# Adding weighted expert rows in memory with an accumulating scatter, in place of a weighted sum after the expert loop

## The chip, the cores and the metric

One core of a Trainium2 chip runs the whole program. The metric is the device time of one execution in microseconds; the kernel before takes 620.18 us (median of 3 runs, 618.78 to 622.79).

## The reference

x has shape (8, 512, 256): 8 sequences of 512 tokens with 256 channels, float32. There are two blocks, each a residual around a normalised sublayer:

```python
x = x + LN(S4D(LN(x)))          # convolution along the sequence, done through a transform, + its own LN
x = x + LN(MoE(LN(x)))          # what this case is about
# MoE(z0):
z = LN(z0) * ln_g + ln_b
probs = softmax(z @ rW + rb)                 # 8 experts, the two best are kept
w = top2(probs) / sum(top2(probs))
hid = gelu(z @ W1[e] + b1[e])                # 256 -> 512
out_e = hid @ W2[e] + b2[e]                  # 512 -> 256
return z0 + sum over the two chosen e of w_e * out_e
```

So each of the 4096 tokens goes through two of eight experts. Before the last LN stands z0 plus two weighted expert rows, z0 being the normalised row itself.

## The kernel before, in words

**Rows and routing.** The first stage works through the 8 sequences in a pipeline (`steps`): transform, multiply, inverse transform, norms. Per sequence b it leaves `xs[b]` (x after the first block, "x1"), stored to `x1_dram` by SyncE's `store_x1`, and `zn[buf(b)]`, the normalised rows with two more columns, the token's number (column H) and its second expert (column H+1). `zn` has four buffers; ScalarE's `renormalise` writes them. VectorE's `choose` and `place` find the two experts of each token and its place in each expert's region, and GpSimd scatters `zn` into `z_rows` (L1121), 128 rows per indirect DMA. Then VectorE makes the table of 71 tiles of 128 rows (`tab`, `tab_e`), sorted by expert, each expert padded to whole tiles with rows that go to a trash area, and the softmax weights `wgt`.

**The expert loop.** `tiles(eng, part)` writes the same software pipeline for each engine: part i handles tile i+2 in its first step, i+1 in its second, i in its third and i-1 in its last. Parts -2 to 2 and the last three are written out, the others run in a hardware loop of 6 parts per turn (`UNROLL`), whose turn costs a branch and, on TensorE and VectorE, register loads of the expert's number (L295). Each engine executes its own list in order, and semaphores tie the lists together. For one part:
- TensorE: transpose the rows (L1321), first layer (L1334), transpose the hidden rows (L1343), second layer (L1353). The layers run as three products of high and low parts.
- ScalarE: `z_f`, the rows with gain and bias (L587), tile i+2; the high part of the transposed hidden rows, `h_hl` (L595), tile i; GELU (L601), tile i+1.
- VectorE: flag (L1010) and destination (L1013) of tile i+2, then the two halves of `z_hl` (L1018, L1020); `hb` = first layer + bias (L1028), tile i+1; low part of `h_hl` (L1033), tile i; index copy `dst` (L1042) and `y_sb` = second layer + bias (L1043), tile i-1.
- GpSimd: `scatter_y` writes `y_sb` by `dst` to `y_rows` (L1157), 2 x 4096 rows, first and second choice apart. Each scatter waits until the one before has landed.
- SyncE loads the next tile's rows (L383).

`gate(eng)` is an increment of a semaphore of its own that stands between a wait and the instruction after it. `do` issues an instruction and waits for its end.

**The tail.** SyncE waits for all scatters, then loads for n = 0 to 7 both choices of a sequence (`ya`, L413, 2 x 512 KB), with the 2 MB of x1 of the other four sequences in between (L411). GpSimd builds `diag`, diagonal matrices of the weights (L1171); TensorE sums the two choices with them (L1369); ScalarE has computed z0 anew from x1 into `acc` (`base`, L610); VectorE adds both (L1053), takes the statistics (L1057, L1062), ScalarE the square root (L617), VectorE scale and shift (L1067 to L1073), ScalarE normalises (L621), VectorE adds x1 (L1079), SyncE stores (L417).

## Time and profile before

| what | value |
|---|---|
| time of the profiled execution | 619.86 us |
| its span, first to last instruction | 618.0 us |
| mean granted clock of TensorE | 0.899 |
| TensorE matmuls busy | 483.4 us, 78% |
| TensorE weight loads busy | 418.9 us, 68% |
| VectorE busy | 463.6 us, 75% |
| ScalarE busy | 347.2 us, 56% |
| GpSimd busy | 223.7 us, 36% |
| moved by DMA | 69.57 MB |

The 1.9 us between span and time lie around the instructions. By the slices of the page, the first stage reaches to about 250 us, the end of routing to 290, the expert loop to 548, the tail from there to 618. Register, branch and semaphore instructions are not counted as busy. The ends of matmuls are modelled, so TensorE's starts are a better measure than its ends. A wait called "issue" is one for which the profile shows no cause.

### The profile page before, as it was taken

Reading aid. Unit: us, or ns where it says so; the run is one execution under the profiler, and the core shown is the slowest. Engines: PE = TensorE matmul, PEld = TensorE weight load, DVE = VectorE, ACT = ScalarE, POOL = GpSimd, SP = SyncE. Lnnn points to the kernel's source line nnn. Section 1 sums busy time; section 2 is a strip of 40 time slices with the busy share of each in tenths; the row PEclk is TensorE's granted clock in tenths of the full one; section 3 lists DMA queues with packets and bytes.
Section 4 is the critical chain, followed back from the end, with each engine's and each line's share of the span. In section 5 each row is a group of like instructions: output and inputs, shape, how many; then the busy total and the mean of one; then the engine's idle time right before and its main releaser. Section 6 shows DMA issues by size and latency. Waiting matters only on the chain. (4 is left out here: it accounts for less than half of the span.)

```text
span 618.0 us, 12460 instructions
## 1 busy us (share of the span) xinstructions
PE 483.4 (78%) x2841; PEld 418.9 (68%) x2842; DVE 463.6 (75%) x1412; ACT 347.2 (56%) x751; POOL 223.7 (36%) x195
## 2 busy tenths in 40 slices
PE   0379899869979774131999999999999999947860
PEld 0129888759868673130798898888888988946740
DVE  6998787997886963864677777777778777732885
ACT  6992755654855567431555555555555555560584
POOL 0000666337675763652032232232232322342410
PEclk9997999989989975555899999999999999987885
DMA  6206600101111788245522222222222222219833
GB/s 173 102 0 250 227 1 1 68 2 69 43 53 43 274 270 286 94 133 143 175 75 80 68 77 77 68 81 72 68 76 77 69 79 74 60 45 367 300 148 136
DMA packets 37260, 69.57 MB, mean 113 GB/s; under 512 B 7568, under 2 KB 23696, under 8 KB 36720
## 3 DMA queue, kind: packets, MB, share of 16 engines
q1 hardware_dynamic: 30752, 51.48, 25.7%
q0 software_dynamic: 6480, 17.77, 8.1%
q8 instruction: 11, 0.18, 0.1%
q14 instruction: 17, 0.14, 0.1%
HBM read 42.02 MB, written 27.21 MB: 112 GB/s over the span
## 5 line engine op out<-in xcount | busy, mean ns | idle before, releaser
L1157 POOL DMA_INDIRECT y_rows<-y_sb,dst x71 | 74.6, 1051 | 195.5 <-DVE y_sb L1043 145.2
L1334 PE MATMUL psum<-ws,z_hl 128*128 x426 | 119.7, 417 | 0.6 <-DVE z_hl L1020 0.6
L1353 PE MATMUL psum<-ws,h_hl 128*128 x852 | 116.2, 286 | 0.0
L1353 PEld LDWEIGHTS psum<-ws,h_hl 128*128 128x128 f32 x852 | 103.8, 189 | 0.2 <-issue 0.2
L1121 POOL DMA_INDIRECT z_rows<-zn,pos x64 | 73.4, 1147 | 41.5 <-DVE pos L881 25.0
L1334 PEld LDWEIGHTS psum<-ws,z_hl 128*128 128x128 f32 x426 | 76.7, 192 | 15.8 <-issue 1.3
L595 ACT CAST h_hl<-psum 128x512 fp32r<-128x512 f32 x71 | 41.7, 587 | 74.0 <-PE psum L1343 73.8
L1028 DVE TENSOR_TENSOR hb<-psum,b1r 128x512 f32<-128x512 f32 x71 | 49.1, 692 | 35.9 <-issue 33.4
L587 ACT ACTIVATE z_f<-psum,gb 128x128 f32<-128x128 f32 x142 | 57.0, 451 | 15.6 <-PE psum L1321 13.6
L601 ACT ACTIVATE hg<-hb 128x512 f32<-128x512 f32 x71 | 44.9, 632 | 35.3 <-DVE hb L1028 34.6
L1224 PE MATMUL psum<-pm,ft 128*128 128x256 f32 x256 | 60.5, 396 | 0.4 <-DVE tmp L840 0.4
L1253 PE MATMUL psum<-yf,it 128*128 128x256 f32 x256 | 59.4, 387 | 0.0
L1224 PEld LDWEIGHTS psum<-pm,ft 128*128 128x128 f32 x256 | 50.4, 199 | 8.3 <-issue 1.1
L1253 PEld LDWEIGHTS psum<-yf,it 128*128 128x128 f32 x256 | 48.6, 194 | 6.5 <-POOL yf L1108 0.2
L1033 DVE TENSOR_TENSOR h_hl<-psum,h_hl 128x512 fp32r<-128x512 f32 x71 | 48.4, 681 | 0.7 <-ACT h_hl L595 0.7
L1369 PE MATMUL psum<-ya,diag 128*128 (+1 forms) x128 | 34.5, 437 | 17.8 <-DMA ya<-y_rows 11.9
L1321 PE MATMUL psum<-ident,z_in 128*128 128x128 f32 x142 | 28.5, 283 | 20.4 <-DMA z_in<-z_rows 18.6
L1369 PEld LDWEIGHTS psum<-ya,diag 128*128 128x128 f32 x128 | 28.1, 222 | 24.0 <-issue 19.2
L1343 PE MATMUL psum<-ident,hg 128*128 128x128 f32 x284 | 42.7, 273 | 0.0
L1343 PEld LDWEIGHTS psum<-ident,hg 128*128 128x128 f32 x284 | 35.5, 141 | 10.0 <-issue 0.2
L1106 POOL TENSOR_TENSOR yf<-yf,tmp 128x512 f32<-128x512 f32 x16 | 20.4, 1276 | 40.8 <-DVE rs L933 24.3
L1114 POOL TENSOR_TENSOR pm<-xn 128x512 f32<-128x512 f32 x8 | 10.3, 1287 | 67.4 <-ACT xn L444 67.4
(205 smaller groups left out, 850.2 us busy)
## 6 DMA issues: line engine op xcount, KB each, us to landing
z_in<-z_rows SPq DMA_DIRECT2D x71, 129.0 KB
w_raw<-in_dram SPq DMA_DIRECT2D x16, 512.0 KB, 5.5
ya<-y_rows SPq DMA_DIRECT2D x16, 512.0 KB, 6.1
xs<-in_dram SPq DMA_DIRECT2D x8, 512.0 KB, 5.7
x_dram<-xs SPq DMA_DIRECT2D x8, 512.0 KB
out_dram<-acc SPq DMA_DIRECT2D x8, 512.0 KB, 2.6
b1r<-in_dram SPq DMA_DIRECT2D x8, 256.0 KB
x1m<-x_dram SPq DMA_DIRECT2D x4, 512.0 KB
```

The source lines that it names most:

```text
L587: last = nc.scalar.activation(z_f[:, k], ps_z[q][:, k], ACT.Identity, bias=gb[:, 1, k:k + 1], scale=gb[:, 0, k:k + 1])
L601: nc.scalar.activation(hg[q][:, :], hb[:, :], ACT.Gelu).then_inc(sem("hg_ready"), 1)
L1028: V.tensor_tensor(hb[:, :], ps_h[q], b1r[:, bass.ds(e, 1)].rearrange("p a f -> p (a f)"), ALU.add).then_inc(sem("hb_ready"), 1)
L1033: V.tensor_tensor(h_hl[q][:, 1], ps_t[q], h_hl[q][:, 0].bitcast(F32), ALU.subtract).then_inc(sem("h_split"), 1)
L1121: pool.indirect_dma_start(z_rows, bass.IndirectOffsetOnAxis(ap=pos[row.par][:, i // 4, i % 4:i % 4 + 1], axis=0), zn[buf(row.b)][:, i % 4] ...
L1157: pool.indirect_dma_start(y_rows, bass.IndirectOffsetOnAxis(ap=dst[q][:, 0:1], axis=0), y_sb[q][:, :], None).then_inc(sem(f"y_out{q}"), 16)
L1224: last = TE.matmul(fw[u][c][:, k], ft[:, c, t, kt * P:(kt + 1) * P], pm[row.b][:, c, t], start=t == 0, stop=t == 1)
L1253: last = TE.matmul(iv[c][:, j * H:(j + 1) * H], it[:, c, k, j * P:(j + 1) * P], yf[row.par][:, c, k], start=k == 0, stop=k == KT - 1)
L1334: last = TE.matmul(ps_h[q], z_hl[q][:, a, k], w_at(e1, c, k * F, F), start=n == 0, stop=n == 5)
L1343: last = TE.transpose(ps_t[q][:, k], hg[q][:, k * P:(k + 1) * P], ident[:, :])
L1353: last = TE.matmul(ps_y[q], h_hl[q][:, a, k], w_at(e2, c, 1024 + k * H, H), start=n == 0, stop=n == 11)
L1369: last = TE.matmul(ps_mix[par][:, k * H:(k + 1) * H], diag[par][:, c, k], ya[:, bass.ds(n, 1), c, k].rearrange("p a h -> p (a h)"), start= ...
```

## The change

The sum over the two experts is made in memory. `y_rows` now has 4096 rows (and two trash blocks of 128), and SyncE stores the normalised rows z0 there in the first stage (`store_rows`). Its order changes: the stores no longer come after the last forward transform; expert 4's weights come after expert 5's. The softmax weights are stored to a small table `w_rows` (4 bytes per token and choice). In the loop, GpSimd gathers the 128 weights of tile t+4 after the scatter of tile t (`gather_w`), with the index `widx` that VectorE writes; ScalarE multiplies `y_sb` by them into `yw` (three buffers) as a fourth step for tile i-2; and GpSimd's scatter adds `yw` to the rows in memory. The two choices of a token lie in different experts, so two scatters of the same expert never meet in a row. VectorE computes for each tile (`order`) whether it may follow the scatter two back, or, at a change of expert, must wait until the one before has landed. ScalarE's first loop turn is written out (`peel`). The tail loads the finished sums once (`yr`), takes the statistics, normalises, adds x1 on GpSimd (the last half block on VectorE). The mean and variance and the shift lie in PSUM. `diag`, the mix on TensorE, `base`, and the two additions before the statistics are gone.

```diff
-TRASH = 2 * B * T
+TRASH = B * T
...
-    dest = at("dest", [P, TILES + 1], U32, c0 + 6240)
-    dst = [at(f"dst{i}", [P, 1], U32, c0 + 6528 + 32 * i) for i in range(2)]
+    dst = [at(f"dst{i}", [P, 1], U32, o0 + 71 * KB + 256 + 32 * i) for i in range(6)]
+    row_of = at("row_of", [P, TILES + 1], U32, o0 + 71 * KB + 448)
+    order = at("order", [1, TILES + 1], I32, o0 + 71 * KB + 736)
+    widx = [at(f"widx{i}", [P, 1], U32, o0 + 71 * KB + 32 * i) for i in range(2)]
+    wt = [at(f"wt{i}", [P, 1], F32, o0 + 71 * KB + 64 + 32 * i) for i in range(6)]
+    yw = [at(f"yw{i}", [P, H], F32, o0 + k * KB) for i, k in enumerate((69, 70, 49))]
...
+    mvm = [bank(i)[:, 0:8].rearrange("p (k c) -> p k c", k=4) for i in range(2)]
+    m_shift = [bank(2 + i)[:, 0:4] for i in range(2)]
...
-    y_rows = nc.dram_tensor("y_rows", [TRASH + P, H], F32, kind="Internal").ap()
+    y_rows = nc.dram_tensor("y_rows", [B * T + 2 * P, H], F32, kind="Internal").ap()
+    w_rows = nc.dram_tensor("w_rows", [2 * B * T, 1], F32, kind="Internal").ap()
...
-    def tiles(eng, part):
+    def tiles(eng, part, peel=0):
         loaded[eng.engine.name] = {}
-        for i in range(-2, 3):
+        for i in range(-2, 3 + UNROLL * peel):
             part(i, i % 2, i)
-        with eng.Fori(0, (TILES - 5) // UNROLL) as j:
+        with eng.Fori(peel, (TILES - 5) // UNROLL) as j:
...
+    def slot(t, u, ahead):
+        return (t if isinstance(t, int) else u + 3 + ahead) % UNROLL
...
+            def store_rows(lo, hi):
+                for b in range(lo, hi):
+                    sp.wait_ge(sem("x1_ready"), b + 1)
+                    sp.dma_start(x1_dram[:, b], xs[b][:, :, :]).then_inc(sem("x1_stored"), 16)
+                    sp.wait_ge(sem("zn_ready"), b + 1)
+                    sp.dma_start(y_tok[:, b], zn[buf(b)][:, :, 0:H]).then_inc(sem(f"zn_stored{buf(b)}"), 16)
+                sp.wait_ge(sem("x1_stored"), 16 * hi)
+            store_rows(0, 4)
+            load_expert(sp, 5)
+            store_rows(4, 5)
             sp.wait_ge(sem("kf_mm"), 2)
             sp.wait_ge(sem("fwd_mm"), 16)
             load_expert(sp, 4)
...
+            for q in range(2):
+                sp.dma_start(y_rows[TRASH + q * P:TRASH + q * P + P, :], zpad[:, 0:H]).then_inc(sem("trash_set"), 16)
...
+            sp.wait_ge(sem("wgt_ready"), 1)
+            sp.dma_start(w_rows.rearrange("(c p n) o -> p c (n o)", c=2, p=P),
+                         wgt[:, 0:2].rearrange("p c b k -> p c (b k)")).then_inc(sem("w_stored"), 16)
...
             for n in range(B):
-                if n >= 2:
-                    sp.wait_ge(sem(f"y0_in{n % 2}"), 16 * (n // 2))
-                    sp.wait_ge(sem(f"y1_in{n % 2}"), 16 * (n // 2))
-                if n == 3:
+                if n == 2:
+                    sp.wait_ge(sem("x1_in"), 64)
                     sp.dma_start(x1m[:, 0:4], x1_dram[:, 0:4]).then_inc(sem("x1_in"), 16)
-                for c in (1, 0):
-                    sp.dma_start(ya[:, n, c], y_tok[:, B - 1 - n, c].rearrange("p (k h) -> p k h", k=4)).then_inc(
-                        sem(f"y{c}_in{n % 2}"), 16)
+                sp.dma_start(yr[:, n], y_tok[:, B - 1 - n]).then_inc(sem(f"y_in{n}"), 16)
             for n in range(B):
                 sp.wait_ge(sem("m_out"), n + 1)
+                if n == B - 1:
+                    sp.wait_ge(sem("m_last"), 1)
...
+                    act.wait_ge(sem(f"zn_stored{row.par}"), 8 * (row.b - row.par))
...
+                t, q = i - 2, par
+                if live(t):
+                    act.wait_ge(sem("y_ready"), t + 1)
+                    gate(act)
+                    act.wait_ge(sem(f"w_in{q}"), (t - q) * 8 + 16)
+                    m = slot(t, u, -2)
+                    if not early(t, 3):
+                        act.wait_ge(sem(f"y_out{1 - q}"), (t - 2 + q) * 8)
+                    nc.scalar.activation(yw[m % 3][:, :], y_sb[q][:, :], ACT.Identity, scale=wt[m][:, 0:1]).then_inc(sem("yw_ready"), 1)
+            tiles(act, part, 1)
+            part(TILES + 1, (TILES + 1) % 2, TILES + 1)
...
+            def close(n):
+                act.wait_ge(sem("m_var"), n + 1)
+                nc.scalar.activation(rm[:, n % 2, 0, :], mvm[n % 2][:, :, 1], ACT.Sqrt, bias=eps[:, 0:1]).then_inc(sem("m_sd"), 1)
...
+                    last = nc.scalar.activation(acc[:, n, k], yr[:, n, k], ACT.Identity,
+                                                bias=rm[:, n % 2, 2, k:k + 1], scale=rm[:, n % 2, 1, k:k + 1])
+                    if n == B - 1 and k == 1:
+                        last.then_inc(sem("m_fin"), 1)
...
+            do(V.tensor_tensor(tf[0:1, 1, 1:NT], tab_e[0:1, 1:NT], tab_e[0:1, 0:NT - 1], ALU.is_equal))
+            do(V.scalar_tensor_tensor(tf[0:1, 2, 1:NT], tf[0:1, 1, 1:NT], -16.0, iot[0:1, 2, 1:NT], ALU.mult, ALU.add))
+            V.tensor_scalar(order[0:1, 1:NT], tf[0:1, 2, 1:NT], 16.0, None, ALU.max).then_inc(sem("order_ready"), 1)
...
+                    if q:
+                        V.scalar_tensor_tensor(row_of[:, bass.ds(t, 1)], z_in[q][:, H + 1:W], 0.0, z_in[q][:, H:H + 1], ALU.min, ALU.add)
+                    else:
+                        V.tensor_copy(row_of[:, bass.ds(t, 1)], z_in[q][:, H:H + 1])
                     V.tensor_scalar(flag[:, :], z_in[q][:, H + 1:W], tab_e[:, bass.ds(t, 1)], float(B * T),
                                     ALU.is_equal, ALU.mult).then_inc(sem("flag_set"), 1)
                     dve.wait_ge(sem("flag_set"), t + 1)
-                    V.tensor_tensor(dest[:, bass.ds(t, 1)], z_in[q][:, H:H + 1], flag[:, :],
+                    if not early(t, 2):
+                        dve.wait_ge(sem(f"w_in{q}"), (t - q) * 8)
+                    gate(dve)
+                    V.tensor_tensor(widx[q][:, :], z_in[q][:, H:H + 1], flag[:, :],
                                     ALU.add).then_inc(sem("dest_ready"), 1)
...
-                        dve.wait_ge(sem(f"y_out{q}"), (t - q) * 8)
+                        dve.wait_ge(sem("yw_ready"), t - 1)
                     gate(dve)
-                    V.tensor_copy(dst[q][:, :], dest[:, bass.ds(t, 1)])
+                    V.tensor_copy(dst[slot(t, u, -1)][:, :], row_of[:, bass.ds(t, 1)])
...
+            def spread_of(n):
+                dve.wait_ge(sem(f"y_in{n}"), 16)
+                if n > 1:
+                    dve.wait_ge(sem("m_sd"), n - 1)
...
+                    last = V.bn_stats(st[:, n % 4, k, :], yr[:, n, k])
+                do(last)
                 for k in range(4):
+                    last = V.bn_aggr(mvm[n % 2][:, k, :], st[:, n % 4, k, :])
                 last.then_inc(sem("m_var"), 1)
...
+            def scale(n):
+                par = n % 2
+                dve.wait_ge(sem("m_sd"), n + 1)
+                if n > 1:
+                    dve.wait_ge(sem("m_fin"), n - 1)
+                do(V.reciprocal(rm[:, par, 1, :], rm[:, par, 0, :]))
+                do(V.tensor_tensor(m_shift[par], mvm[par][:, :, 0], rm[:, par, 1, :], ALU.mult))
+                V.tensor_tensor(rm[:, par, 2, :], xb[:, B - 1 - n], m_shift[par], ALU.subtract).then_inc(sem("m_rs"), 1)
+            spread_of(0)
+            for n in range(B):
+                if n + 1 < B:
+                    spread_of(n + 1)
+                scale(n)
+            dve.wait_ge(sem("m_fin"), B + 1)
             dve.wait_ge(sem("x1_in"), 80)
-            with dve.Fori(1, B // 2 - 1) as j:
-                mix(j * 2 + 2, 0)
-                scale(j * 2 + 1, 1)
-                add(j * 2)
-                mix(j * 2 + 3, 1)
-                scale(j * 2 + 2, 0)
-                add(j * 2 + 1)
-            scale(B - 1, 1)
-            add(B - 2)
-            add(B - 1)
+            V.tensor_tensor(acc[:, B - 1, 2:4], acc[:, B - 1, 2:4], x1m[:, 0, 2:4], ALU.add).then_inc(sem("m_last"), 1)
...
+            def gather_w(t, q, m):
+                pool.wait_ge(sem("dest_ready"), t + 1)
+                gate(pool)
+                pool.indirect_dma_start(wt[m][:, 0:1], None, w_rows,
+                                        bass.IndirectOffsetOnAxis(ap=widx[q][:, 0:1], axis=0)).then_inc(sem(f"w_in{q}"), 16)
+            def scatter_y(t, q, m):
                 if not early(t):
-                    pool.wait_ge(sem(f"y_out{1 - q}"), (t + q) * 8)
+                    behind = pool.value_load(order[0:1, bass.ds(t, 1)], min_val=16, max_val=16 * TILES)
+                    pool.wait_ge(sem(f"y_out{1 - q}"), behind)
+                    gate(pool)
+                if not early(t, 2):
+                    pool.wait_ge(sem(f"y_out{q}"), (t - q) * 8)
+                    gate(pool)
+                pool.wait_ge(sem("yw_ready"), t + 1)
                 gate(pool)
-                pool.indirect_dma_start(y_rows, bass.IndirectOffsetOnAxis(ap=dst[q][:, 0:1], axis=0),
-                                        y_sb[q][:, :], None).then_inc(sem(f"y_out{q}"), 16)
-            scatter_y(0, 0)
-            with pool.Fori(0, (TILES - 1) // 2) as j:
-                scatter_y(j * 2 + 1, 1)
-                scatter_y(j * 2 + 2, 0)
-            def weights(n, par):
-                if not early(n, 2):
-                    pool.wait_ge(sem("m_sum"), n - 1)
-                w = wgt[:, 0:2, bass.ds(back(n), 1)].rearrange("p c a k -> p c (a k)")
-                G.tensor_tensor(diag[par][:, :, :, :], ident[:, :].unsqueeze(1).unsqueeze(1).to_broadcast([P, 2, 4, P]),
-                                w.unsqueeze(3).to_broadcast([P, 2, 4, P]), ALU.mult).then_inc(sem("m_diag"), 1)
-            pool.wait_ge(sem("rsm_ready"), 1)
-            pool.wait_ge(sem("hb_ready"), TILES)
-            weights(0, 0)
-            weights(1, 1)
-            with pool.Fori(1, B // 2) as j:
-                weights(j * 2, 0)
-                weights(j * 2 + 1, 1)
+                pool.indirect_dma_start(y_rows, bass.IndirectOffsetOnAxis(ap=dst[m][:, 0:1], axis=0),
+                                        yw[m % 3][:, :], None, compute_op=ALU.add).then_inc(sem(f"y_out{q}"), 16)
+            pool.wait_ge(sem("w_stored"), 16)
+            for t in range(4):
+                gather_w(t, t % 2, t % 6)
+            for b in range(B - 2):
+                pool.wait_ge(sem(f"zn_stored{b % 2}"), 16 * (b // 2 + 1))
+            for i in (2, 3):
+                pool.wait_ge(sem(f"zn_stored{i}"), 16)
+            pool.wait_ge(sem("trash_set"), 32)
+            pool.wait_ge(sem("order_ready"), 1)
+            for t in range(7):
+                scatter_y(t, t % 2, t % 6)
+                gather_w(t + 4, t % 2, (t + 4) % 6)
+            with pool.Fori(1, (TILES - 5) // UNROLL) as j:
+                for u in range(UNROLL):
+                    scatter_y(j * UNROLL + (1 + u), (1 + u) % 2, (1 + u) % 6)
+                    gather_w(j * UNROLL + (5 + u), (1 + u) % 2, (5 + u) % 6)
+            for t in range(TILES - 4, TILES):
+                scatter_y(t, t % 2, t % 6)
+            def add(n, ks):
+                pool.wait_ge(sem("m_fin"), n + 1)
+                if n % 4 == 0:
+                    pool.wait_ge(sem("x1_in"), 80 if n else 64)
+                G.tensor_tensor(acc[:, n, ks], acc[:, n, ks], x1m[:, B - 1 - n, ks], ALU.add).then_inc(sem("m_out"), 1)
+            for n in range(B):
+                add(n, slice(0, 2 if n == B - 1 else 4))
```

## Rows read from the trace of the kernel before

**Rows 1.** Busy time by stretch: busy us (instructions) per engine, granted clock, DMA share, GB/s.

```profile
450.00:500.00 50.00, 49.66 (x338) 44.19 (x337) 39.34 (x114) 27.87 (x58) 14.61 (x14) 1.00 0.24 74
...
560.00:570.00 10.00, 9.63 (x33) 8.13 (x34) 3.01 (x9) 0.02 (x1) 1.90 (x1) 0.73 1.01 376
```

**Rows 2.** ScalarE's longest wait in the loop, 330 to 530: total us, times, longest.

```profile
ACT h_hl L595 <- PE psum L1343: 60.4, 57, 1.2
```

**Rows 3.** Timeline of VectorE in the loop: start us, length us, instruction, idle before it.

```profile
430.48 0.69 DVE L1028 TENSOR_TENSOR hb<-psum,b1r 128x512 f32<-128x512 f32 x1 [0.49 <-issue]
...
439.48 0.15 DVE L1042 COPY dst<-dest 128x1 uint32 x1 [0.42 <-issue]
...
441.65 0.69 DVE L1028 TENSOR_TENSOR hb<-psum,b1r 128x512 f32<-128x512 f32 x1 [0.51 <-issue]
...
443.27 0.20 DVE L1010 TENSOR_SCALAR flag<-z_in,tab_e 128x1 f32<-128x1 f32 x1
...
443.74 0.29 DVE L1018 CAST z_hl<-z_f 128x256 fp32r<-128x256 f32 x1
...
444.99 0.69 DVE L1028 TENSOR_TENSOR hb<-psum,b1r 128x512 f32<-128x512 f32 x1 [0.50 <-issue]
...
451.79 0.69 DVE L1028 TENSOR_TENSOR hb<-psum,b1r 128x512 f32<-128x512 f32 x1 [0.51 <-issue]
```

**Rows 4.** Timeline of ScalarE in the loop.

```profile
442.38 0.63 ACT L601 ACTIVATE hg<-hb 128x512 f32<-128x512 f32 x1 [0.60 <-DVE hb L1028]
442.91 0.79 ACT L587 ACTIVATE z_f<-psum,gb 128x128 f32<-128x128 f32 x2
```

**Rows 5.** Timeline of the TensorE weight loads in the loop.

```profile
440.88 1.45 PEld L1353 LDWEIGHTS psum<-ws,h_hl 128*128 128x128 f32 x12
...
444.32 1.45 PEld L1353 LDWEIGHTS psum<-ws,h_hl 128*128 128x128 f32 x12
```

**Rows 6.** ScalarE on 128x256: four in a row; a group: busy us, mean ns.

```profile
259.21 2.08 ACT L519 ACTIVATE zn<-xs,rs 128x256 f32<-128x256 f32 x4
...
L467 ACT ACTIVATE tq<-qt,phase 128x256 f32<-128x256 f32 x16 | 6.5, 493 | 0.0
```

**Rows 7.** Timeline of GpSimd outside and in the loop, with the y_sb it waits for.

```profile
274.06 0.98 POOL L1121 DMA_INDIRECT z_rows<-zn,pos  x1 [0.30 <-issue]
...
446.37 0.42 DVE L1043 TENSOR_TENSOR y_sb<-psum,b2r 128x256 f32<-128x256 f32 x1
...
447.61 1.12 POOL L1157 DMA_INDIRECT y_rows<-y_sb,dst  x1 [2.29 <-DVE y_sb L1043]
```

**Rows 8.** DMA of L1157 from 380 to 540 us, and of L413: issue to landing.

```profile
L1157 POOL DMA_INDIRECT y_rows<-y_sb,dst x46: 958/1074/1131, 380.4 to 539.6; - x46
...
DMA to landing us min/median/max: 2.4/2.5/2.7
...
DMA to landing us min/median/max: 3.7/6.1/11.5
```

**Rows 9.** Timeline of the tail, and GpSimd on half a block (L1106).

```profile
555.21 5.83 SPq L413 DMA_DIRECT2D ya<-y_rows  x6
...
568.02 1.40 DVE L1057 BATCH_NORM_STATS2 st<-acc 128x6 f32<-128x256 f32 x4
...
569.98 0.30 ACT L617 ACTIVATE rm<-mvm,eps 128x4 f32<-128x4 f32 x1 [12.69 <-DVE mvm L1062]
...
610.62 0.28 ACT L617 ACTIVATE rm<-mvm,eps 128x4 f32<-128x4 f32 x1
...
611.45 0.16 DVE L1073 TENSOR_TENSOR rm<-rm,xb 128x4 f32<-128x4 f32 x1 [0.15 <-DVE rm L1069]
...
611.65 2.07 ACT L621 ACTIVATE acc<-acc,rm 128x256 f32<-128x256 f32 x4 [0.76 <-DVE rm L1073]
613.76 1.23 DVE L1079 TENSOR_TENSOR acc<-acc,x1m 128x1024 f32<-128x1024 f32 x1 [1.00 <-ACT acc L621]
...
L1106 POOL TENSOR_TENSOR yf<-yf,tmp x16: 1265/1277/1286, 81.5 to 215.8; 128x512 f32<-128x512 f32 x16
```

More of the change, by code:

```diff
@@ L179, in program @@
     tf = at("tf", [P, 3, TILES + 1], F32, o0 + 63 * KB)
[L180 to L182 removed]
+    iot = at("iot", [P, 3, TILES + 1], F32, o0 + 65 * KB)
+    yr = at("yr", [P, B, 4, H], F32, 0)
     acc = at("acc", [P, B, 4, H], F32, 64 * KB)
@@ L277, in back @@
         return n * -1 + (B - 1)
-    ps_mix = [bank(2 * i, 2) for i in range(2)]
+    y_tok = y_rows[0:TRASH, :].rearrange("(p b k) h -> p b k h", b=B, k=4)
     def route(b):
@@ L572, in _ @@
             act.wait_ge(sem("pad_set"), 1)
-            nc.scalar.activation(rsm[:, 0], mv1[:, :, :, 1], ACT.Sqrt, bias=eps[:, 0:1], scale=1.0 / H).then_inc(sem("rsm_sd"), 1)
             act.wait_ge(sem("wsm_sub"), 1)
@@ L601, in part @@
                     nc.scalar.activation(hg[q][:, :], hb[:, :], ACT.Gelu).then_inc(sem("hg_ready"), 1)
-            tiles(act, part)
-            def base(n):
-                b = back(n)
-                for k in range(4):
-                    last = nc.scalar.activation(acc[:, bass.ds(n, 1), k].rearrange("p a h -> p (a h)"),
-                                                x1m[:, bass.ds(b, 1), k].rearrange("p a h -> p (a h)"), ACT.Identity,
-                                                bias=rsm[:, 1, bass.ds(b, 1), k], scale=rsm[:, 0, bass.ds(b, 1), k])
-                last.then_inc(sem("m_base"), 1)
@@ L615, in close @@
-            def close(b, par):
-                act.wait_ge(sem("m_var"), b + 1)
-                nc.scalar.activation(rm[:, par, 0, :], mvm[par][:, :, 1], ACT.Sqrt, bias=eps[:, 0:1]).then_inc(sem("m_sd"), 1)
-                act.wait_ge(sem("m_rs"), b + 1)
-                for k in range(4):
-                    row = acc[:, bass.ds(b, 1), k].rearrange("p a h -> p (a h)")
-                    last = nc.scalar.activation(row, row, ACT.Identity,
-                                                bias=rm[:, par, 2, k:k + 1], scale=rm[:, par, 1, k:k + 1])
-                last.then_inc(sem("m_fin"), 1)
@@ L1182, in _ @@
+            for n in range(B):
+                add(n, slice(0, 2 if n == B - 1 else 4))
         @block.tensor
@@ L1358, in _ @@
             tiles(pe, part)
-            def mix(n, par):
-                pe.wait_ge(sem("m_diag"), n + 1)
-                pe.wait_ge(sem(f"y1_in{par}"), n * 8 + 16 - 8 * par)
-                pe.wait_ge(sem(f"y0_in{par}"), n * 8 + 16 - 8 * par)
-                if not early(n, 2):
-                    pe.wait_ge(sem("m_mixed"), n - 1)
-                for k in range(4):
-                    for c in (1, 0):
-                        last = TE.matmul(ps_mix[par][:, k * H:(k + 1) * H], diag[par][:, c, k],
-                                         ya[:, bass.ds(n, 1), c, k].rearrange("p a h -> p (a h)"),
-                                         start=c == 1, stop=c == 0)
-                last.then_inc(sem("m_sum"), 1)
-            pe.wait_ge(sem("y_ready"), TILES)
-            mix(0, 0)
-            mix(1, 1)
-            with pe.Fori(1, B // 2) as j:
-                mix(j * 2, 0)
-                mix(j * 2 + 1, 1)
 def fine(i):
```

100 lines of the change are left out of this document (16 added, 84 removed).

## Prediction

> **What bounds the kernel now.** The time busy by stretch comes first. It shows two stages that the change touches: the loop over 71 tiles, with TensorE busy all the time at full clock, and the tail, in which the DMA queues are full [rows 1]. The waits of the loop come next: ScalarE waits for TensorE, 60.4 us in 57 times [rows 2], while TensorE has no row of note. TensorE's share alone would say that nothing else matters there. The timelines say otherwise. TensorE's second layer starts every 3.44 us [rows 5]. VectorE repeats after 3.34 us where it does not stand for TensorE (its hb add starts at 441.65 and 444.99), and six tiles, one turn of the unrolled loop, take 451.79 - 430.48 = 21.31 us, or 3.55 each; that is 0.6 more than six times 3.44, spent at the turn of the loop [rows 3].
>
> The 3.34 us are a ring of two engines, read off one after the other [rows 3, 4]: hb add at 441.65, GELU at 442.38 (0.73), z_f at 442.91 (0.53), its two halves done and the cast on VectorE at 443.74 (0.83), the next hb add at 444.99 (1.25). Each waits for the one before it, by data or by its place in its engine's program. So it has 0.10 us of slack against TensorE, although ScalarE's busy share is only 56%. A new instruction between GELU and z_f goes into this ring.
>
> **The change, part by part.**
> *Weighting on ScalarE.* One 128x256 Identity with a scale per partition per tile stands at the end of ScalarE's part, after GELU and ahead of the next z_f: in the ring. Four such operations with bias and scale take 2.08 us where one takes 0.59, thus 0.50 each; sixteen with bias alone take 6.5 us, 0.41 each [rows 6]. I take 0.46. The ring becomes 3.34 + 0.46 = 3.80 us, past TensorE's 3.44.
>
> *VectorE.* Per tile one more 128x1 operation (0.20, as the flag row [rows 3]) and a wait with a gate; 0.35 together. VectorE's own way from hb to the cast takes 2.09 us, as does the way over ScalarE, which grows to 2.55, so 2.44 hides under it. Once per turn VectorE loads one register more (0.42 [rows 3]) and takes the branch: these are not hidden any more, 0.3 and 0.2. The turn is 6 x 3.80 + 0.5 = 23.3 us, 2.0 more than now.
>
> *GpSimd.* Now one indirect DMA per tile; then two, four gates and a register load. A gated scatter starts 0.82 us after its data (y_sb is done at 446.79, it starts at 447.61); two without gates follow each other with 0.30 between them [rows 7]. So a gate with its wait costs some 0.54. The queue's own work per tile is 1.07 + 0.30 + 1.07 + 0.30 = 2.7 us of issuing; the gates and the load (4 x 0.54 + 0.5) add as much again if nothing overlaps (5.4 us), nothing if all is hidden (2.7). I take 3.6, because a wait can be worked on while an indirect DMA is made, as the landing waits are now.
>
> *A second ring, through the gathered weight.* VectorE may overwrite the index of tile t only when the gather of t-2 has landed, and that gather stands behind the scatter of t-6 on the queue. Over two tiles: scatter after its weighting 0.82, gather behind it 1.3, landing 2.5 (that of the present scatter [rows 8]; a smaller transfer may need less), index and cast 0.35, then 1.25 + 0.73 + 0.53 + 0.50 to the next weighting but one. The sum is 8.0 us, 4.0 per tile, against 3.80 of the first ring. With a landing of 2.0 it is 3.74. The Trainium skill (DMA: Bandwidth & Descriptors, Anatomy of one DMA) gives a GpSimd-issued DMA some 2.0 us plus its bytes at 436 GB/s: by that 3.74 holds and the first ring decides. I go between them, 3.88 per tile, and a turn of 23.7 us: 2.4 more than now, and 2.4 x 71/6 = +28 us.
>
> *The accumulating scatter.* No row shows one. From below it lands like the plain one, 2.5 us after its start [rows 8]; from above after twice that, since each row is also read. I take 3.3. Within an expert two may be in flight, so up to 6 us would be hidden. At each of the seven changes of expert the scatter waits for the one before: 3.3, then three gates at 0.54 and 0.3 to the start, 5.2 us against 3.9, so 1.3 late, with hardly any slack in the second ring. +7 us, between 2 and 20.
>
> *GpSimd's port.* Indirect issues take 1.07 us in the loop and 0.96 to 0.98 outside it [rows 7, 8]. The Trainium skill (SBUF — State Buffer, the box on DVE blocking DMA) has a copy on VectorE lock GpSimd out of writing descriptors until it ends; the row shows 0.1 us of something like it per issue, and by the rule a second issue per tile could lose as much as the 0.29 us cast. That would only eat the slack of the queue.
>
> *Before the loop.* The normalised rows are stored once more (8 x 512 KB), two trash blocks and the weights too. The stores of x1 no longer stand behind the forward transforms. ScalarE gets four waits for them, a step or more late. All of it lies beside the rows' pipeline. The weights' store stands between the loads of the first tiles: +0.5 us.
>
> *The tail.* Now it runs from the first load of y at 555.21 to the end at 618.0, 62.8 us [rows 9]. Eight mixes on TensorE, the base on ScalarE and one addition on VectorE go; the last addition moves to GpSimd. What remains: the first 512 KB land after 3.7 us (the shortest landing [rows 8]); statistics to the square root 1.96 (568.02 to 569.98); square root to the first normalisation 1.03, less 0.11 of the 0.15 that stands ahead of L1073 behind a gate, then 2.07: the first block is normalised at 8.7. Each further block costs 2.07 + 0.92 - 0.09 of overlap = 2.9 us on ScalarE. But the 2 MB of x1 go out ahead of the third block: at 376 GB/s [rows 1] 5.6 us, so that block lands at 3.7 + 1.4 + 5.6 + 1.4 = 12.1, its statistics end at 14.0, only then is the second block scaled (VectorE's order), normalised at 16.7. Six more make 34.1. GpSimd's addition takes 2.5 us per block (1.28 for half [rows 9]), below 2.9; the last half block ends 1.2 after, and store and end take 3.0, as now from the end of the last add. Together 38.3 us, a gain of 24.5. Without the stall behind x1 it would be 29.5; with additions slowed to 3.5 us, 20. The small operands in PSUM save a gate and nothing else that a row shows.
>
> *The end of the loop.* Weighting plus a slower landing: +1.
>
> **Sum.** 619.9 of the profiled execution (0.3 below the median of 620.2): +28 +7 +0.5 +1 -24.5 = +12, **631 us**. The tail's gain is spent in the loop.
>
> **Rivals.**
> *The loop stays with TensorE's pace.* If the weighting fits into ScalarE's idle time (over 1 us before its h_hl cast, 60 us in 57 waits [rows 2]) and the gathers are early, the loop costs at most what 0.31 of extra ring costs, +10, at best nothing: 619.9 + 0 to 10 + 1.5 - 24.5 = 597 to 607 us. For it speaks the large idle time, against it that this idle time lies on the other side of z_f: it is waited out anyway after z_f has been handed over. It decides if the ring stays below 3.6.
> *GpSimd's queue becomes the pace.* If gates do not overlap with the issues (5.4 us per tile) or the accumulating scatter takes 6 us and more, a tile takes 4.5 to 5.4: (4.5 - 3.55) x 71 = +67, and +131 at the upper end: 664 to 728 us. For it: seven queue steps in place of two. Against it: 3.6 leaves 0.3. It decides from 4.0 per tile.
> *Only the first ring, no late scatters*: +24 +2 +1.5 -24.5 gives 623, within my case.
>
> **Chances.** My case, loop at 3.75 to 4.05 per tile, 0.58: its own range is 620 to 643. TensorE's pace or near it 0.22, GpSimd's 0.20. The range of 8 in 10 takes in most of both: 604 to 662. What this measurement can tell from no change is 1%, 613.9 to 626.3. Faster takes the first rival and little else, 0.23; same, the lower third of my case, 0.20; slower 0.57.
>
> **What the profile would show.** The hb adds six tiles apart stand 23 to 24.5 us apart; z_f begins later after GELU by the new ScalarE line's 0.4 to 0.5; TensorE now waits in the loop, some 0.4 us per tile, still at full clock; scatters at seven places over 5 us apart. VectorE's index operation waits for DMA. In the tail no TensorE, first store some 12 us after the first load, end 38 after it. Wrong if the turn stays at 21.3 (first rival), if GpSimd is busy or in its sequencer without a pause and the tile takes over 4.3 (second), or if the tail takes over 45: then GpSimd's additions are slower beside VectorE.

## The result

The changed kernel takes 651.9 us (median of 4 runs, 651.5 to 654.35); the kernel before 620.7 us (median of 4 runs, 618.78 to 622.79). The ratio is 1.052, with a 95% interval of 1.0485 to 1.0557: 31 us slower, where 11 were forecast (631.0 against 620.2). The time lies in the range of 604 to 662 and on the likeliest side, but above the 620 to 643 of the prediction's own case, and the slowing is nearly three times the forecast one. The profiled execution took 652.09 us, with a span of 649.9; it answers to 619.86 and 618.0 of before. The mean granted clock is 0.898 in the one and 0.899 in the other, so the clock takes no part in this comparison.

**The profile after.** First its busy time by stretch, one row from the middle of the loop and one from the tail. The columns are those of [rows 1].

```profile
450.00:500.00 50.00, 44.95 (x277) 35.99 (x277) 32.56 (x105) 25.33 (x57) 30.31 (x24) 1.00 0.37 62
620.00:630.00 10.00, 0.00 (x0) 0.00 (x0) 6.04 (x30) 5.48 (x14) 4.67 (x2) 0.50 0.99 381
```

In the loop TensorE does 277 matmuls in 50 us where it did 338 [rows 1], still at full clock. GpSimd is busy twice as long, but idle for 40%: no engine is full. In the tail TensorE has nothing to do; its clock stands at the lower level (0.50), which costs nothing there, and the DMA queues are as full as before.

The span splits at three marks: the first hb addition, the last one, and the first load of y in the tail. Times are from the trace's timelines, in us.

| stretch | before | after | difference |
|---|---|---|---|
| start to the first hb | 296.3 | 295.7 | -0.6 |
| first hb to the last (70 tiles on) | 246.8 | 300.9 | +54.1 |
| last hb to the first load of y | 12.1 | 15.1 | +3.0 |
| first load to the end | 62.8 | 38.1 | -24.7 |

The sum is +31.9, the difference of the spans. The tail gave what was forecast (-24.5). The loop cost 54 us where 28 + 7 were forecast.

**Where the loop waits.** The longest waits between 330 and 560 us, by engine, instruction and releaser: total us, times, longest.

```profile
ACT hg L613 <- DVE hb L1035: 84.2, 42, 3.3
DVE widx L1020 <- DMA wt<-w_rows,widx: 50.1, 51, 2.0
POOL y_rows L1155 <- DVE widx L1020: 40.3, 20, 2.6
```

ScalarE's wait for TensorE [rows 2] is gone from the head of the list. It now waits for VectorE's hb, and VectorE waits for a DMA, in nearly every tile: its index of tile t may be written only when the gather of t-2 has landed. GpSimd's scatter waits in turn for ScalarE's weighting and, in 20 cases by the profile, for the index. Read together these are a ring, closed over three engines and a DMA. One turn of it in the timeline, 439 to 449 us, with the instructions of the ring alone (start, length, instruction, idle before it):

```profile
439.44 0.49 ACT L622 ACTIVATE yw<-y_sb,wt 128x256 f32<-128x256 f32 x1
...
440.74 1.59 POOL L1155 DMA_INDIRECT y_rows<-yw,dst  x1 [2.14 <-ACT yw L622]
...
442.63 0.97 POOL L1141 DMA_INDIRECT wt<-w_rows,widx  x1 [0.30 <-issue]
...
445.15 0.16 DVE L1020 TENSOR_TENSOR widx<-z_in,flag 128x1 uint32<-128x1 f32 x1 [1.21 <-DMA wt<-w_rows,widx]
445.26 0.64 DVE L1025 CAST z_hl<-z_f 128x256 fp32r<-128x256 f32 x1
...
446.86 0.69 DVE L1035 TENSOR_TENSOR hb<-psum,b1r 128x512 f32<-128x512 f32 x1 [0.51 <-issue]
...
447.59 0.63 ACT L613 ACTIVATE hg<-hb 128x512 f32<-128x512 f32 x1 [2.09 <-issue]
...
448.12 0.49 ACT L622 ACTIVATE yw<-y_sb,wt 128x256 f32<-128x256 f32 x1
```

Follow it down. The weighting of one tile ends at 439.93; its scatter starts at 440.74 and holds GpSimd for 1.59 us. Only then can the gather behind it in the program be made, 442.63. It lands in time for the index at 445.15, 1.21 us after VectorE could have written it. The cast of z stands behind the index in VectorE's program and waits with it, then hb, GELU, and the next weighting but one at 448.12. That is 8.7 us from weighting to weighting, for two tiles. The two tiles of a pair are not alike: the index of one waits long for its gather (2.01, 1.76 and 1.21 us at 428.07, 436.80 and 445.15), that of the other little (0.22 and 0.64 at 431.53 and 440.68). In the timeline of VectorE just before, the hb additions stand 3.74 and 4.99 us apart.

```profile
429.44 0.69 DVE L1035 TENSOR_TENSOR hb<-psum,b1r 128x512 f32<-128x512 f32 x1 [0.51 <-issue]
...
433.18 0.69 DVE L1035 TENSOR_TENSOR hb<-psum,b1r 128x512 f32<-128x512 f32 x1 [0.50 <-issue]
...
438.17 0.69 DVE L1035 TENSOR_TENSOR hb<-psum,b1r 128x512 f32<-128x512 f32 x1 [0.51 <-issue]
```

The short one, 3.74, is the first ring with the weighting in it. The weighting's own cost is seen beside [rows 4], where z_f began 0.53 after GELU. In the timeline of ScalarE now, yw begins 0.53 after GELU and z_f another 0.40 on.

```profile
430.17 0.63 ACT L613 ACTIVATE hg<-hb 128x512 f32<-128x512 f32 x1 [3.05 <-DVE hb L1035]
...
430.70 0.49 ACT L622 ACTIVATE yw<-y_sb,wt 128x256 f32<-128x256 f32 x1
...
431.10 0.78 ACT L599 ACTIVATE z_f<-psum,gb 128x128 f32<-128x128 f32 x2
```

**The tail**, timeline rows that answer to [rows 9]:

```profile
607.89 1.55 POOL L1155 DMA_INDIRECT y_rows<-yw,dst  x1 [0.86 <-DMA y_rows<-yw,dst]
611.81 0.81 SPq L424 DMA_DIRECT2D yr<-y_rows  x2
612.67 0.42 SPq L423 DMA_DIRECT2D x1m<-x_dram  x1
613.13 3.22 SPq L424 DMA_DIRECT2D yr<-y_rows  x6
...
619.41 2.08 ACT L633 ACTIVATE acc<-yr,rm 128x256 f32<-128x256 f32 x4 [1.90 <-DVE rm L1074]
...
621.57 2.33 POOL L1181 TENSOR_TENSOR acc<-acc,x1m 128x1024 f32<-128x1024 f32 x1 [12.13 <-ACT acc L633]
623.19 1.41 DVE L1061 BATCH_NORM_STATS2 st<-yr 128x6 f32<-128x256 f32 x4 [3.81 <-DMA yr<-y_rows]
...
625.51 2.07 ACT L633 ACTIVATE acc<-yr,rm 128x256 f32<-128x256 f32 x4 [3.87 <-DVE rm L1074]
...
628.37 2.07 ACT L633 ACTIVATE acc<-yr,rm 128x256 f32<-128x256 f32 x4 [0.64 <-DVE rm L1074]
...
631.24 2.07 ACT L633 ACTIVATE acc<-yr,rm 128x256 f32<-128x256 f32 x4 [0.64 <-DVE rm L1074]
```

The third block of y comes late behind the 2 MB of x1, and VectorE stands for 3.81 us; from then on a block takes 2.87 us. The load at 611.81 stands 3.9 us behind the start of the last scatter.

### The profile page after: what moved, and what is told of

It is laid out like the page before. It is cut to its first block, busy times and chain, and to the rows that moved or that the text cites. A ratio compares the mean times of both kernels' runs of the same rounds, so it can differ in the third digit from the quotient of the medians.

```text
span 649.9 us, 12865 instructions
## 1 busy us (share of the span) xinstructions
PE 472.5 (73%) x2713; PEld 389.3 (60%) x2714; DVE 444.6 (68%) x1469; ACT 347.7 (53%) x788; POOL 335.4 (52%) x267
## 4 chain that ended last, share of the span: by engine, by line
DMA 22%; DVE 20%; issue 17%; PE 14%; ACT 13%; POOL 7%; POOLq 3%; DVEq 1%; SPq 1%; ACTq 0%
DMA y_rows<-yw,dst 11%; DMA wt<-w_rows,widx 8%; PE psum L1257 3%; POOL y_rows L1155 3%; PE psum L1228 3%; POOLq L1147 2%; ACT acc L633 2%; POOL wt L1141 2%; ACT yw L622 2%; DVE hb L1035 2%; DMA yr<-y_rows 2%; PE psum L1215 1%; ACT dump L518 1%; ACT dump L562 1%; PE psum L1204 1%
## 5 line engine op out<-in xcount | busy, mean ns | idle before, releaser
L1155 POOL DMA_INDIRECT y_rows<-yw,dst x71 | 114.1, 1607 | 106.2 <-DVE widx L1020 54.2
L1141 POOL DMA_INDIRECT wt<-w_rows,widx x71 | 70.1, 987 | 36.2 <-issue 20.9
L1020 DVE TENSOR_TENSOR widx<-z_in,flag 128x1 uint32<-128x1 f32 x71 | 11.4, 160 | 67.1 <-DMA wt<-w_rows,widx 64.3
L1257 PEld LDWEIGHTS psum<-yf,it 128*128 128x128 f32 x256 | 48.5, 194 | 6.4 <-POOL yf L1094 0.2
L1347 PE MATMUL psum<-ident,hg 128*128 128x128 f32 x284 | 44.7, 280 | 3.3 <-ACT hg L613 0.2
L1347 PEld LDWEIGHTS psum<-ident,hg 128*128 128x128 f32 x284 | 31.6, 141 | 24.1 <-ACT hg L613 20.5
```

The costliest lines, as they stand in the source:

```text
L1141: pool.indirect_dma_start(wt[m][:, 0:1], None, w_rows, bass.IndirectOffsetOnAxis(ap=widx[q][:, 0:1], axis=0)).then_inc(sem(f"w_in{q}"), 16)
L1155: pool.indirect_dma_start(y_rows, bass.IndirectOffsetOnAxis(ap=dst[m][:, 0:1], axis=0), yw[m % 3][:, :], None, compute_op=ALU.add).then_in ...
L1257: last = TE.matmul(iv[c][:, j * H:(j + 1) * H], it[:, c, k, j * P:(j + 1) * P], yf[row.par][:, c, k], start=k == 0, stop=k == KT - 1)
L1347: last = TE.transpose(ps_t[q][:, k], hg[q][:, k * P:(k + 1) * P], ident[:, :])
```

## The experiments

Three theories of the loop's 4.36 us per tile (mean distance of the hb additions from the 9th tile to the 63rd; 3.55 before). **A**: the ring weighting, scatter, gather, index, cast, hb, GELU, that is, the order of two DMAs on GpSimd's queue. **B**: the adding scatters land slowly and pace the loop themselves. **C**: GpSimd's own instructions do, its waits and gates included. Here is what the changed kernel and ten variants of it gave; "per tile" is the same mean for each. Each was timed beside the kernel before, in three groups, each on a chip of its own: e1 to e4, e5 to e8, e9 and e10. The kernel before had medians of 620.7, 620.8 and 620.8 us in them, so kernels of different groups can be set side by side. A few us of the medians are not the loop's, though: in the profiled executions the first hb addition comes between 295.7 us (after) and 301.7 (e6), though no edit changes the first stage. The granted clock is 0.97 from 100 to 200 us in before, after, e2, e3 and e7, and 0.91 to 0.93 in the others; the three latest starts (e1, e6, e10, 300.8 and later) also have only 0.95 in the first 100 us. In the loop, 300 to 540 us, it is 0.99 or 1.00 in every kernel, so the time per tile is free of it.

| kernel | edit to the changed kernel | median us (lowest to highest) | ratio to before, 95% | per tile |
|---|---|---|---|---|
| after | none | 651.9 (651.5 to 654.35) | 1.0485 to 1.0557 | 4.36 |
| e1 | six index buffers | 613.9 (612.2 to 615.9) | 0.981 to 0.994 | 3.77 |
| e2 | weighting earlier | 606.1 (605.7 to 608.0) | 0.970 to 0.983 | 3.67 |
| e3 | e1 and e2 | 604.9 (602.5 to 605.9) | 0.968 to 0.981 | 3.63 |
| e4 | scatter writes, doesn't add | 622.5 (619.6 to 625.2) | 0.9985 to 1.0056 | 3.95 |
| e5 | gather ahead of scatter | 617.4 (614.5 to 619.4) | 0.992 to 0.997 | 3.78 |
| e6 | every scatter waits for the last | 699.4 (698.1 to 701.3) | 1.121 to 1.133 | 4.90 |
| e7 | x1 behind the blocks of y | 650.5 (648.5 to 654.3) | 1.044 to 1.057 | 4.35 |
| e8 | e3 and e7 | 607.0 (605.5 to 609.9) | 0.974 to 0.985 | 3.74 |
| e9 | e3, e5 and e7 | 601.8 (594.9 to 603.8) | 0.960 to 0.975 | 3.63 |
| e10 | e3, one gate for three | 603.9 (602.9 to 606.2) | 0.970 to 0.975 | 3.65 |

**e1, six index buffers.** VectorE's write of an index waits for the gather of six tiles ago, not of two.

```
-    widx = [at(f"widx{i}", [P, 1], U32, ...) for i in range(2)]
+    widx = [at(f"widx{i}", [P, 1], U32, ...) for i in range(UNROLL)]
...
-                    if not early(t, 2):
-                        dve.wait_ge(sem(f"w_in{q}"), (t - q) * 8)
+                    m = slot(t, u, 2)
+                    if not early(t, UNROLL):
+                        dve.wait_ge(sem(f"w_in{m}"), nth(t, u, 2) * 16)
```

> Six buffers for the gather's index in place of two, each with its own semaphore; VectorE's first loop turn is written out. Theory A (the ring through the index: weighting, scatter, gather, landing, index, hb, GELU, weighting two tiles on, 8.7 us per two tiles) says that VectorE now waits for a gather three rounds back, the ring is gone and ScalarE's ring of 3.34 + 0.5 us is next: 3.85 to 3.95 us per tile, 652 - 0.45 x 70 = 620 us. Theory B (the accumulating scatters' landing paces the loop) says no change, 652. Theory C (GpSimd's own work per tile, two issues and the gates between them, paces it) says at most a few us less, 645 and over.

Measured: 613.9 us and 3.77 per tile. That is below the 3.85 to 3.95 expected, which took the weighting as 0.5 and not as 0.40. VectorE's wait for the gather is gone from the list of waits; the first ring, 3.34 + 0.40 = 3.74, is what is left. The same adding scatters and the same GpSimd instructions now run at 3.77, so neither B nor C can have set 4.36.

**e2, the weighting earlier.** ScalarE's line moves from behind GELU to behind z_f, ahead of the h_hl cast; both index buffers stay two.

```
+                t, q = i - 2, par
+                if live(t):
+                    act.wait_ge(sem("y_ready"), t + 1)
...
+                    nc.scalar.activation(yw[m % 3][:, :], y_sb[q][:, :], ACT.Identity, ...)
...
-                    nc.scalar.activation(yw[m % 3][:, :], y_sb[q][:, :], ACT.Identity, ...)
```

> Only ScalarE's weighting moves, from behind GELU to just behind z_f of the same part. Theory A: the weighting no longer stands behind hb and GELU of its part, the ring through the index now spans three tiles (about 9.5 us, 3.2 per tile) and ScalarE's own ring is back at 3.34; the loop is then paced by TensorE (3.55) or by GpSimd's shortest cycle (1.92 from scatter to gather, 1.76 from gather to scatter, 3.7 us): 608 us, between 600 and 612. Theory B: no change, 652. Theory C, if GpSimd's cycle were the pace already: 645 and over.

Measured: 606.1 us, 3.67 per tile. The edit puts the weighting behind z_f and ahead of the h_hl cast, where ScalarE stands for TensorE anyway (it still does, 26.7 us in 52 times from 330 to 560). It also starts each scatter earlier in its tile, so that the gather behind it has mostly landed when the index is due: VectorE's wait for it is down from 50.1 us in 51 times to 3.0 in 5. That the gain is larger than in e1 fits both rings being shorter; no run parts the two.

**e3, both.**

> Both edits together. Theory A: as the weighting moved alone, since either edit breaks the ring: 608 us; what is left over 3.55 us per tile is GpSimd's cycle of 3.7. Theory B: 652.

Measured: 604.9 us, 3.63 per tile. Busy time by stretch and the longest waits of this kernel, as above:

```profile
450.00:500.00 50.00, 48.52 (x334) 43.41 (x332) 38.30 (x126) 32.64 (x70) 34.80 (x28) 1.00 0.45 71
```

```profile
ACT hg L629 <- DVE hb L1043: 44.0, 60, 1.3
DVE hb L1043 <- issue: 31.5, 60, 0.8
ACT h_hl L623 <- PE psum L1355: 28.4, 59, 0.7
```

TensorE is busy for 48.5 of 50 us with 334 matmuls, against 49.66 and 338 before the change [rows 1]. No wait for a DMA is among the longest, and ScalarE's wait for TensorE ahead of the h_hl cast is 28.4 us where the kernel before has 65.8 from 330 to 560 us (60.4 up to 530 [rows 2]): the weighting stands in it. The loop is near TensorE's pace with all the scatters and gathers of the change in it. The last 0.08 us per tile against 3.55, some 6 us, is not explained by a run.

**e4, the scatter writes and does not add.** The additions of the rows are left out, nothing else.

```
-                                        yw[m % 3][:, :], None, compute_op=ALU.add)...
+                                        yw[m % 3][:, :], None)...
```

> The scatter writes instead of adding; the additions in memory are left out, all else stays. Theory A with the scatter's longer issue as the mis-sized term: the issue falls from 1.6 us to about 1.05, the ring loses 0.55 to 0.6 us per two tiles, 0.3 us per tile: 631 us. Theory B (landing of the adding scatter): the loop falls to 3.9 us per tile or below, 620 us. If the addition costs nothing: 652.

Measured: 622.5 us, 3.95 per tile: 29 us less than the changed kernel. That is 8 below what theory A expected and near what B did (620 us, 3.9 or below), for this edit shortens the issue and the landing together; alone it would not part A from B. e1 and e5 do. The DMA view of its scatter between 380 and 540 us (engine, operation, count: length in ns min/median/max):

```profile
L1155 POOL DMA_INDIRECT y_rows<-yw,dst x40: 983/984/1101, 381.2 to 536.0; - x40
...
DMA to landing us min/median/max: 2.4/2.8/3.3
```

and of the changed kernel:

```profile
L1155 POOL DMA_INDIRECT y_rows<-yw,dst x37: 1579/1586/1826, 379.2 to 535.6; - x37
```

The adding form holds GpSimd 0.60 us longer per scatter, and the gather stands right behind it: from scatter to gather 1.36 us here, 1.92 there (means of 48 tiles). In the ring 0.56 counts once in two tiles, 0.28 per tile; 0.41 was gained, so some 0.1 per tile comes from elsewhere: the ring's other links are shorter by another 0.23 or so in two tiles (gather to index 2.50 against 2.62, cast to hb 1.26 against 1.32, weighting to scatter 0.85 against 0.91). A faster landing can show in the first and the last of these, not in the scatter-to-gather link.

**e5, the gather ahead of the scatter.** Two calls change places on GpSimd, in the hardware loop as below and in the seven tiles written out ahead of it.

```
...
                 for u in range(UNROLL):
-                    scatter_y(j * UNROLL + (1 + u), (1 + u) % 2, (1 + u) % 6)
                     gather_w(j * UNROLL + (5 + u), (1 + u) % 2, (5 + u) % 6)
+                    scatter_y(j * UNROLL + (1 + u), (1 + u) % 2, (1 + u) % 6)
```

> One edit: on GpSimd's queue the gather of the weights of tile t+4 is issued ahead of the scatter of tile t, in place of behind it. Nothing else moves. Theory A (the pace of 4.36 us per tile is the ring scatter, gather behind it, index, cast, hb, GELU, weighting): the index of the next tile but one no longer stands behind a scatter that waits for the weighting, so the ring is broken; ScalarE's own ring of 3.34 + 0.40 = 3.74 us is left. Loop 71 x (3.75 to 3.9), so 652 - 71 x (0.45 to 0.6) = 609 to 620 us; VectorE's index operation waits for DMA under 0.5 us, not 1.2. Theory B (the landing of the accumulating scatters paces the loop) and theory C (GpSimd's own instructions pace it): the same instructions and the same transfers in another order, so 652 us, within 1%.

Measured: 617.4 us, 3.78 per tile. Its longest waits in the loop:

```profile
ACT hg L613 <- DVE hb L1035: 54.2, 47, 1.5
DVE hb L1035 <- issue: 30.7, 61, 0.5
POOL y_rows L1155 <- issue: 25.5, 30, 2.1
```

VectorE's wait for the gather, 50 us before, is not among them, nor further down the list. This is the sharpest of the tests: no instruction, buffer or byte is different from the changed kernel, and 34.5 us are gone. A alone says so.

**e6, every scatter waits.** GpSimd waits for the landing of the scatter before in each tile, not at the first of an expert alone (and needs no register load for it).

```
-                    behind = pool.value_load(order[0:1, bass.ds(t, 1)], ...)
-                    pool.wait_ge(sem(f"y_out{1 - q}"), behind)
+                    pool.wait_ge(sem(f"y_out{1 - q}"), (t + q) * 8)
```

> Every accumulating scatter waits for the landing of the one before it, not only the first of an expert. Measures the landing of an accumulating scatter and what the wait by expert saves. From the changes of expert, where two scatters stand 5.0 us apart: the pace is landing plus gates plus issue, 5.0 us per tile or a little more with the gather between, so 652 + 71 x (5.0 to 5.4 - 4.36) = 697 to 726 us. If the landing were already the pace in the kernel after (theory B), 652 us within 2%. By theory A alone, with landings hidden beside the ring, it would be 652 as well if a landing took under 3 us.

Measured: 699.4 us, 4.90 per tile, at the lower end of what was expected. With one scatter in flight its landing can be read, in the DMA view of its scatter between 380 and 540 us:

```profile
L1154 POOL DMA_INDIRECT y_rows<-yw,dst x32: 1580/1587/1823, 383.0 to 535.5; - x32
...
DMA to landing us min/median/max: 3.8/3.9/4.1
```

An adding scatter lands 3.9 us after its issue begins; the remaining 1.0 of the pitch are GpSimd's gates and waits. The pitch is even, 4.74 to 5.19 us from scatter to scatter in the loop, so B does describe a kernel, this one. In the changed kernel the wait by expert lets two be in flight, and is worth 47 us against waiting every time.

**e7, x1 last.** SyncE puts the 2 MB of x1 behind all eight blocks of y.

> In the tail, the 2 MB of x1 are put on SyncE's queue behind all eight blocks of y and not ahead of the third. In the profile after VectorE stands 3.81 us for the third block of y. If that stall is passed on to the end: -4 to -5 us, 647 to 648 us. If GpSimd's additions then wait for x1 (2 MB at 376 GB/s, 5.6 us, landing last) or the x1 half becomes what is late: 650 to 655 us.

Measured: 650.5 us. In its profile VectorE no longer stands at the third block, and the tail takes 611.26 to 646.3, 35.0 us against 38.1: 3.1 gained, of the 3.8 it stood. In the medians 1.4 is left, and the runs of the two kernels overlap (648.5 to 654.3, 651.5 to 654.35). A gain is seen in the trace and not proven in the time. The median falls in the expected 650 to 655, but the sign of that branch, additions of GpSimd that wait for x1, is not in the trace: they wait for ScalarE.

**e8, e3 with x1 last.**

> The first two edits of before together (six index buffers, weighting ahead of GELU's wait) and x1 behind the blocks of y. Expected from the parts: 604.9 less 4 to 5 us, 600 us. If the loop's end hides the tail's stall: 604 us.

Measured: 607.0 us, neither the 600 nor the 604 expected, 2 above e3. The tail gained again (568.6 to 604.2, 35.6 us; 38.4 in e3), but the loop took 3.74 per tile against 3.63 with the same instructions in it, both at full clock. I have no cause for that; it stays open. It shows that two kernels whose loops are the same can differ by 6.5 us in it, so the ranking of e3, e8, e9 and e10 among themselves is not settled.

**e9, all four edits.**

> All four edits together: six index buffers, the weighting ahead of GELU's wait, x1 behind the blocks of y, the gather ahead of the scatter on GpSimd's queue. With the ring through the index already gone the order of GpSimd's two transfers should no longer matter, and the loop is at TensorE's pace and the turn's own cost, 3.6 to 3.7 us per tile: 600 to 607 us. If GpSimd's scatter waits less by it, 600; if the gather's wait for the index delays the scatter, over 610.

Measured: 601.8 us, ratio 0.968 (0.960 to 0.975), the fastest: 3.2% below the kernel before, 50 us below the changed one. Loop 3.63, tail 35.6. Against e3, whose loop differs from it by the order of scatter and gather alone, the pace is the same, as expected. Against e8, its neighbour by that one edit, it is not: 3.63 and 3.74 per tile, 601.8 and 607.0 us. That is the open difference of e8 again, so whether the order is still worth something once the index ring is gone is not settled.

**e10, one gate in place of three** ahead of each scatter, on e3.

```
                     pool.wait_ge(sem(f"y_out{1 - q}"), behind)
-                    gate(pool)
                 if not early(t, 2):
                     pool.wait_ge(sem(f"y_out{q}"), (t - q) * 8)
-                    gate(pool)
                 pool.wait_ge(sem("yw_ready"), t + 1)
                 gate(pool)
```

> The kernel with six index buffers and the early weighting, with one gate instead of three ahead of each scatter on GpSimd. Two gates less are 1.1 us per tile if they count in full. Theory C (GpSimd's own instructions pace the loop once the ring is gone, at 3.63 us per tile): the loop drops to 3.5 us or less, 605 - 71 x 0.13 = 596 us or less. If TensorE or ScalarE paces it: 603 to 606 us. At a change of expert the scatter then starts up to 1.1 us earlier, seven times, and hidden as before.

Measured: 603.9 us, 3.65 per tile. The gates that it takes away were idle time that overlapped with waiting: GpSimd now stands for the landing of earlier scatters, 20.1 us in 16 times, where e3 shows 4.2 in 3. GpSimd is not the pace at 3.63 either.

## Why the prediction was right in kind and wrong in size

**The ring of ScalarE: right.** Forecast +0.46 for the weighting and a ring of 3.80; measured +0.40 and 3.74. The kernels without the second ring run at it (e1 3.77, e5 3.78). VectorE's extra work was hidden beside ScalarE as the prediction had it: in e1 all of it is still there. The 0.5 us that it added per turn of the loop is hardly seen: most turns of e1 take 22.5 us, and 6 x 3.74 is 22.4.

**The ring through the gathered index: the right mechanism, two errors of size.** This is the step that failed: its link from scatter to gather was put at 1.3 us and took 1.92, and its sum of 4.0 per tile was then taken as 3.88; the pace was 4.36. Its terms, forecast and as means over 48 tiles of the changed kernel:

| link | forecast | measured |
|---|---|---|
| weighting's end to scatter | 0.82 | 0.91 |
| scatter to gather | 1.3 | 1.92 |
| gather to index | 2.5 | 2.62 |
| index to cast, cast to hb | 0.35 + 1.25 | 0.17 + 1.32 |
| hb to GELU to weighting | 0.73 + 0.53 | 0.74 + 0.54 |
| weighting | 0.50 | 0.49 |
| sum for two tiles | 8.0 | 8.7 |
| per tile | 4.0, taken as 3.88 | 4.36 |

The measured links follow each other without a gap, so that they add up to two tiles proves nothing; that the ring sets the pace is what e1, e2 and e5 show.

The first error: the issue of an adding scatter was priced by the plain one (1.07 us [rows 8]), without even a bound of its own, where the landing was given one. It takes 1.59, and the whole of the difference stands in the ring: 0.3 per tile, some 21 us over 71 tiles. e4 shows it from the other side: with the plain form the scatter-to-gather link falls to 1.36 and the tile to 3.95, where the prediction's own sum said 4.0. The second error: the sum came out at 4.0 and 3.88 was taken, half way to 3.74. That step leaned on a landing of 2.0 for the small gather. The Trainium skill (DMA: Bandwidth & Descriptors, Anatomy of one DMA) has some 2.0 us for it. The measured link from gather to index, 2.62 us on average and at least 2.37, went with the nearest row of before (2.5 [rows 8]). The row should have had the last word: 0.12 x 71 = 8.5 us. With both mended the sum is 8.0 + 0.6 = 8.6 for two tiles; the median distance of a scatter from the last but one, away from the changes of expert, is 8.55. That makes (4.3 - 3.55) x 71 = 53 us. The changes of expert add to it (below), and the first and last tiles, not yet or no longer held by the ring, give some 3 us back: 54.1 measured. The forecast of 28 + 7 also held some 6 us for the turn that did not come.

**Seven changes of expert, +7: right in kind, somewhat less in size.** The prediction had a landing of 3.3 and 1.3 us late each. The landing is 3.9 (e6), and the scatter behind such a wait starts 4.8 to 5.2 us after the last one in the changed kernel, 4.8 to 5.3 in e3 and e9. Its link from weighting to scatter is longer there than the 0.82 of other tiles by 1.33, 1.03, 1.35, 1.19, 0.08, 0.29 and 0.42 us, 5.7 in all. From the two-tile distances, a mean of 8.71 over tiles 10 to 61 and of 8.59 without each change and the three tiles behind it, some 4 us of the loop are theirs, by estimate. In e1 the same scatters start 1.9 to 2.1 us after their weighting, and the loop keeps the first ring's pace: the lateness costs only where the ring hands it on. No run took these waits out, so their cost is estimated, not measured.

**GpSimd's own work: less than forecast.** The shortest distance of two scatters in e3 is 3.17 us, which is 1.59 + 0.30 + 0.98 + 0.30: the gates vanish in it. The prediction took 3.6. (Its price of a gate, 0.54, is 0.82 - 0.30 = 0.52 by its own rows.) Its second rival (4.5 and more per tile) gave a pace close to the measured one by another mechanism, and of its two signs one came: a tile over 4.3, but not a GpSimd without a pause. e1 and e5 rule that mechanism out, since the same instructions run at 3.77. **GpSimd's port** was taken at nothing, and little is seen: the gather's issue takes 0.98 us in the median (0.975 to 1.144) beside VectorE's work in the loop, as the plain form does outside it [rows 7] and, in the median, in the loop of e4. The median of 1.07 in the loop before [rows 8] did not come back in e4; why is open. The adding issue has a median of 1.66 in e1 and e5, 1.59 in the other kernels that add.

**TensorE's pace as the rival of the other side: wrong for this kernel**, and what e3 and e9 reach. It had the condition right, "the gathers are early"; they are not, because they stand behind a scatter. Its upper end does not follow from its own figure: 0.31 us more per tile is 22 us over 71 tiles, not 10.

**The tail: right**, 38.1 us against 38.3, stall behind x1 included (the 2.9 per block was 2.87, GpSimd's addition 2.33 for 2.5). **Before the loop** -0.6 for +0.5. **The loop's end** +3.0 for +1: the first load of y starts 3.9 us after the last scatter does, where it was 2.5 (552.67 to 555.21), 1.4 of it; the other 1.6 lies between the last hb and that scatter, where two weightings wait for the landing of a scatter (2.48 and 1.68 us by the profile). **The sum** as the prediction wrote it is 619.9 + 12 = 631.9, not 631.

## What to carry to other kernels

Where two DMAs share an engine's program, ask what each holds up: a small early transfer that stands behind one waiting for late data inherits its lateness, and turns an innocent double buffer into a ring; putting it ahead, or giving it more buffers, cost nothing here. When a sum of a ring comes out of rows, keep it, and price each new form of an instruction (here the adding scatter) from both sides for every time it has, the issue as well as the landing. ScalarE, busy 56% of the time, had 0.10 us per tile to spare in its ring: place new work where an engine waits for the slowest one, as e2 did.

## What the runs showed of the hardware

An indirect DMA of 128 rows of 1 KB from GpSimd takes 0.98 us to issue when it writes and 1.59 us when it adds (medians of e4 and after), and lands 2.4 to 3.3 us (e4, up to two in flight) and 3.8 to 4.1 us (e6, one in flight) after that begins. The Trainium skill (DMA: Bandwidth & Descriptors, Anatomy of one DMA) has 2.0 us plus the bytes at 436 GB/s, by which an estimate for 128 KB is 2.3 us; the traces are 0.1 to 1.0 us above it for the writing form (median 2.8), and 1.6 us for the adding one (median 3.9). The gather of 128 single words is used 2.62 us after its start on average (after, 2.37 at least), about as late as a plain scatter of 128 KB lands (2.5 [rows 8], 2.8 in e4). Taking away two gates per tile on GpSimd moved nothing that shows (e3 and e10, 604.9 and 603.9 us).
